# The last layer norm of a graph kernel moved from a closing block on VectorE into the tile loop on GpSimd

## The reference, cut to what matters

```python
h = relu(layernorm(x)); Xf = Xb = Xa = h; Z = 0
for s in range(2):                       # step zero and step one
    A = adj_from_feats(Xa, W1, W2, W3)   # logits, keep the top 0.9 of the softmax mass per row
    Xf, Xb, Xa = Rf @ Xf, Rb @ Xb, A @ Xa
    Z = Z + (Xf @ U1[s] + Xb @ U2[s] + Xa @ U3[s])
Y = h + Z
out = x + (Y - mean(Y)) / sqrt(var(Y) + 1e-5) * gamma + beta
```

## Time and profile before

| | us |
|---|---|
| median of 3 runs | 2197.3 (2192.13 to 2199.02) |
| the profiled execution, its own time | 2191.76 |
| its span, first to last instruction | 2190.0 |
| VectorE busy | 1913.4 (87%) |
| TensorE busy | 1880.3 (86%) |
| ScalarE busy | 1680.4 (77%) |
| GpSimd busy | 706.6 (32%) |

### The profile page before, as it was taken

The page is one execution under the profiler, slowest core; times in us unless marked ns, Lnnn a source line. Parts: engine busy times, 40 slices in busy tenths (PEclk is TensorE's granted clock), DMA queues, the critical chain, the costliest instruction groups (busy, mean ns, idle before and its releaser), DMA issues. The chain is left out here.

```text
span 2190.0 us, 32462 instructions
## 1 busy us (share of the span) xinstructions
PE 1880.3 (86%) x9866; PEld 1245.4 (57%) x9866; DVE 1913.4 (87%) x6109; ACT 1680.4 (77%) x1740; POOL 706.6 (32%) x1392
## 2 busy tenths in 40 slices
PE   1999963999999999999883898999899999999892
PEld 1555531666666666666661555666565656565662
DVE  6777788899889999988758999999999999999995
ACT  5444345899999999999824999898989898989940
POOL 2000042244443344444323333333333333333324
PEclk9999986999999999999995999999999999999996
DMA  6777621111111111111106001010101010101023
GB/s 218 284 284 283 217 95 44 38 39 50 54 54 51 55 55 37 52 54 51 55 29 237 21 26 41 23 44 23 44 23 44 23 44 23 44 23 44 22 91 122
DMA packets 65725, 167.61 MB, mean 77 GB/s; under 512 B 7037, under 2 KB 45307, under 8 KB 61947
## 3 DMA queue, kind: packets, MB, share of 16 engines
q1 hardware_dynamic: 65530, 165.43, 21.7%
HBM read 117.95 MB, written 47.45 MB: 76 GB/s over the span
## 5 line engine op out<-in xcount | busy, mean ns | idle before, releaser
L1449 PE MATMUL banks<-xa,pt 128*128 128x256 f32 x2704 | 636.4, 387 | 16.2 <-ACT pt L949 15.8
L1449 PEld LDWEIGHTS banks<-xa,pt 128*128 128x128 f32 x2704 | 501.7, 192 | 157.1 <-issue 71.3
L920 ACT ACTIVATE junk_a<-pb_all,minus_t 128x3327 f16<-128x3327 f32 x150 | 461.0, 3073 | 96.5 <-POOLq L843 93.8
L925 ACT ACTIVATE junk_a<-pb_all,minus_t 128x3327 f16<-128x3327 f32 x150 | 460.6, 3071 | 4.1
L1500 PE MATMUL banks<-region,at 128*128 128x512 f16 x2028 | 456.3, 380 | 0.0
L828 POOL TENSOR_SCALAR over<-over,points 128x1 f32<-128x1 f32 x150 | 96.8, 646 | 763.7 <-ACT junk_a L925 763.7
L1500 PEld LDWEIGHTS banks<-region,at 128*128 128x128 f16 x2028 | 196.4, 98 | 218.3 <-issue 2.1
L1375 PE MATMUL banks<-keys,qs 64*128 64x512 f32 (+1 forms) x816 | 191.2, 569 | 101.0 <-DMA qs<-q_d 31.8
L1241 DVE TENSOR_SCALAR_CACHE_REDUCE pb_all<-banks 128x1024 f32<-128x1024 f32 x260 | 209.3, 848 | 27.4 <-PE banks L1375 19.1
L1103 DVE MAX8 junk_v<-below 128x8 f32<-128x208 f32 (+1 forms) x624 | 222.4, 432 | 2.2
L949 ACT ACTIVATE pt<-banks 128x896 f32<-128x896 f32 x208 | 171.2, 859 | 61.4 <-PE banks L1441 61.2
(11 more groups left out here) (223 smaller groups left out, 2797.8 us busy)
## 6 DMA issues: line engine op xcount, KB each, us to landing
at<-adjT_d SPq DMA_DIRECT2D x52, 832.0 KB, 4.9
region<-in_adj_dram SPq DMA_DIRECT2D x25, 1663.5 KB, 8.0
adjT_d<-at SPq DMA_DIRECT2D x26, 832.0 KB, 3.9
fb_d<-fb_sb SPq DMA_DIRECT2D x26, 256.0 KB, 2.0
region<-fb_d SPq DMA_DIRECT2D x2, 3328.0 KB, 19.2
y_d<-y_sb SPq DMA_DIRECT2D x50, 128.0 KB, 1.7
x_d<-pb_all SPq DMA_DIRECT2D x1, 3328.0 KB, 11.0
qs<-q_d SPq DMA_DIRECT2D x104, 32.0 KB, 4.1
```

The lines of the kernel that those rows point to most:

```text
L920: nc.scalar.activation(junk_a[:, 0:w], pb[u][:, 0:w], ACT.Relu, scale=sign, bias=t, accum_out=over[u][:, 0:1])\
L925: nc.scalar.activation(junk_a[:, 0:w], pb[u][:, 0:w], ACT.Sign, scale=sign, bias=t, accum_out=over[u][:, 1:2])\
L1449: last = nc.tensor.matmul(bank[4][:, 0:D], pt[sl][:, t * P:(t + 1) * P], xa[:, t0 + t, :], start=(t0 + t == 0), stop=(t0 + t == T - 1))
```

## The change

Six edits go together.

1. VectorE: `add_z` in step one is followed by a wait on `y_stats` and a `bn_aggr` of that tile alone; `y_done` is raised by the latter.
2. GpSimd: `normalise(i-2)` stands behind `level(j, 4)` in body i: five linked one-column instructions, of which one is a power of -0.5 and the others a Newton step, then one 128x256 `tensor_scalar` that subtracts the mean and multiplies by the inverse deviation. `finish(i-3)` stands ahead of `level(j, 4)`: three 128x256 `tensor_tensor` instructions (residual plus beta, norm times gamma, their sum). One `memset` is added at the start of the step.
3. SP: per tile, `x1` of the tile is loaded from `x1_d` and the finished tile is stored to `out`. The load of step zero's Y stands one body later; the store to `y_d` in step one is gone.
4. SP: gamma and beta are loaded into `scales` (the memory of `fb_sb`) at the start of step one, ahead of the U matrices and the large feature loads.
5. The closing block is gone: VectorE's `finish`, ScalarE's two `Sqrt` instructions, GpSimd's 26 additions of beta, the large reloads and large stores.
6. The last tile is stored in two pieces after `store_out(T-2)`.

```diff
@@ sync, step one
+                def store_out(q):
+                    sp.wait_ge(S("out_sum"), q.t + 1)
+                    for r0, r1 in LAST_ROWS if q.t == T - 1 else [(0, P)]:
+                        sp.dma_start(out[q.t * P + r0:q.t * P + r1, :], n_t[q.slot][r0:r1, :]).then_inc(S2("out_stored")[q.slot], 16)
                     if not first and i.static and i.t == -2:
+                        for n, v in enumerate((gamma, beta)):
+                            sp.dma_start(scales[:, n, :], bc(v)).then_inc(sem("scale_in"), 16)
...
-                    if not first and i.inside(T):
-                        sp.wait_ge(S2("y_stored")[i.slot], 16 * i.use)
-                        sp.dma_start(y_sb[i.slot][:, :], y_d[dyn(i)]).then_inc(S2("y_loaded")[i.slot], 16)
+                    if not first and k.inside(T):
+                        if k.t >= 2:
+                            sp.wait_ge(S("n_done"), k.t - 1)
+                        sp.dma_start(y_sb[k.slot][:, :], y_d[dyn(k)]).then_inc(S2("y_loaded")[k.slot], 16)
+                        if k.t >= 2:
+                            sp.wait_ge(S("out_sum"), k.t - 1)
+                        sp.dma_start(x1_t[k.slot], x1_d[:, k.t * D:(k.t + 1) * D]).then_inc(S2("x1_loaded")[k.slot], 16)
+                    if not first and (i + -3).inside(T):
+                        store_out(i + -3)
...
@@ gpsimd
+                def normalise(q):
+                    pool.wait_ge(S2("y_done")[q.slot], q.use + 1)
+                    mean, var = mv[:, q.t, 0:1], mv[:, q.t, 1:2]
+                    v, root, h, r = (a[:, q.t:q.t + 1] for a in (ve, sd, lt, ly[:, :, 0]))
+                    ch.link(nc.gpsimd.tensor_scalar(v, var, EPS, None, ALU.add))
+                    ch.link(nc.gpsimd.tensor_tensor(root, v, minus_half[:, :], ALU.pow))
+                    ch.link(nc.gpsimd.tensor_scalar(h, root, root, v, ALU.mult, ALU.mult))
+                    ch.link(nc.gpsimd.tensor_scalar(h, h, -0.5, 1.5, ALU.mult, ALU.add))
+                    ch.link(nc.gpsimd.tensor_tensor(r, root, h, ALU.mult))
+                    pool.wait_ge(S2("out_stored")[q.slot], 16 * q.use_here)
+                    nc.gpsimd.tensor_scalar(n_t[q.slot], y_sb[q.slot][:, :], mean, r, ALU.subtract, ALU.mult).then_inc(S("n_done"), 1)
+
+                def finish(q):
+                    pool.wait_ge(S2("x1_loaded")[q.slot], 16 * (q.use_here + 1))
+                    pool.wait_ge(sem("scale_in"), 32)
+                    pool.wait_ge(S("n_done"), q.t + 1)
+                    ch.add(nc.gpsimd.tensor_tensor(x1_t[q.slot], x1_t[q.slot], scales[:, 1, :], ALU.add))
+                    ch.link(nc.gpsimd.tensor_tensor(n_t[q.slot], n_t[q.slot], scales[:, 0, :], ALU.mult))
+                    nc.gpsimd.tensor_tensor(n_t[q.slot], n_t[q.slot], x1_t[q.slot], ALU.add).then_inc(S("out_sum"), 1)
...
+                    if not first and 0 <= i.t - 3 < T - 2:
+                        finish(i + -3)
                     for e in range(EARLY if first else EARLY + 1, SUB + ACT_BISECTIONS[s] - 1):
                         level(j, e)
+                    if not first and (i + -2).inside(T):
+                        normalise(i + -2)
+                        if i.t >= T:
+                            finish(i + -2)
                     if not first:
                         level(m, 0)
...
@@ vector
-                        nc.vector.bn_stats(stats[:, k.t, :], y_sb[k.slot][:, :]).then_inc(S2("y_done")[k.slot], 1)
+                        nc.vector.bn_stats(stats[:, k.t, :], y_sb[k.slot][:, :]).then_inc(S("y_stats"), 1)
+                        dve.wait_ge(S("y_stats"), k.t + 1)
+                        nc.vector.bn_aggr(mv[:, k.t, :], stats[:, k.t, :]).then_inc(S2("y_done")[k.slot], 1)
```

More of the change, by code:

```diff
@@ L341, in sweep @@
             body(Idx(0, i, base, unroll))
-    OUT_GROUPS = [(t, 6) for t in range(0, T - 2, 6)]
     def dyn(i):
@@ L723, in diffusion_step @@
         nxt = Idx(0, 0, T, 6)
+        x1_t = [v[:, 0, :] for v in t256]
+        n_t = [v[:, 1, :] for v in t256]
+        EVEN = LAST - LAST % 16
+        LAST_ROWS = [(r0, r1) for r0, r1 in ((0, EVEN), (EVEN, LAST)) if r1 > r0]
         with nc.Block() as block:
@@ L762, in body @@
                         sp.dma_start(q_d[1, dyn(k)], qo[:, :]).then_inc(S("qo_stored"), 16)
-                    if k.inside(T) and (first or not k.static or k.t < T - 2):
+                    if first and k.inside(T):
                         sp.wait_ge(S2("y_done")[k.slot], k.use + 1)
                         sp.dma_start(y_d[dyn(k)], y_sb[k.slot][:, :]).then_inc(S2("y_stored")[k.slot], 16)
[L766 to L775, removed]
                 step_sweep(sp, body)
@@ L784, in _ @@
                 else:
[L785 to L795, removed]
+                    store_out(Idx(0, T - 1, T, 6))
+                    for u in range(2):
+                        sp.wait_ge(S2("out_stored")[u], 16 * (T // 2 + (len(LAST_ROWS) - 1 if u == (T - 1) % 2 else 0)))
             @block.gpsimd
@@ L848, in _ @@
                 ch = Chain(pool, f"step_levels_{s}")
+                if not first:
+                    ch.link(nc.gpsimd.memset(minus_half[:, :], -0.5))
                 def body(i):
@@ L882, in _ @@
                 step_sweep(pool, body)
[L883 to L887, removed]
             @block.scalar
@@ L1295, in settle @@
                     dve.sem_inc(S("masked"), 1)
[L1297 to L1301, removed]
-                    ch.wait()
-                    inverse_deviation(dve, 4 if t0 else 3, "out_chain", 6 if t0 else 0, 1.0, t0, t1)
-                    dve.wait_ge(sem("scale_in"), 32)
-                    for h, (u0, n) in enumerate(OUT_GROUPS if t0 == 0 else [(t0, t1 - t0)]):
-                        if t0 == 0:
-                            dve.wait_ge(sem("y_in"), 16 * len(OUT_GROUPS))
-                        for t in range(u0, u0 + n):
-                            y = y_sb[t % 2][:, :] if t0 else yall[:, t, :]
-                            nc.vector.scalar_tensor_tensor(out=yall[:, t, :], in0=y, scalar=mv[:, t, 0:1], in1=gamma_bc,
-                                                           op0=ALU.subtract, op1=ALU.mult).then_inc(sem("out_scaled"), 1)
-                        dve.wait_ge(sem("out_scaled"), u0 + n)
-                        dve.wait_ge(sem("x1_beta"), u0 + n)
-                        for t in range(u0, u0 + n):
-                            nc.vector.scalar_tensor_tensor(out=yall[:, t, :], in0=yall[:, t, :], scalar=ly[:, t, :], in1=x1_in[:, t, :],
-                                                           op0=ALU.mult, op1=ALU.add).then_inc(sem("out_done"), 1)
                 def coarse_search(j):
@@ L1347, in body @@
                             coarse_search(nxt)
-                    if not first and i.static and i.t == T - 1:
-                        for u in range(2):
-                            dve.wait_ge(S2("y_done")[u], T - 1)
-                        finish(0, T - 2)
                 step_sweep(dve, body)
-                if not first:
-                    for u in range(2):
-                        dve.wait_ge(S2("y_done")[u], T)
-                    finish(T - 2, T)
             @block.tensor
```

10 lines of the change are left out of this document (2 added, 8 removed).

## The result

The changed kernel takes 2171.95 us (median of four runs, 2170.07 to 2178.67) against 2197.85 us for the kernel before (median of four, 2192.13 to 2199.02). The ratio is 0.989, 95% interval 0.987 to 0.991; a later set, with six runs of the one and 17 of the other, gives 0.989 again, 0.987 to 0.991. The forecast was 2178.4, in a range from 2170 to 2192.

The account below looks back on a forecast made before the run. VectorE's own list was taken to set the tile's period of 37.0 us. Terms: -30.0 close, +9.6 loop, +0.6 body 25, +0.9 start = -18.9 us; 2197.3 - 18.9 = 2178.4 us, range 2170 to 2192.

Parts of the forecast that it names:

- the band of 2176 to 2183: Whole kernel: forecast case, each tile 0.3 to 0.6 us longer on VectorE; chance 0.55.
- the aggregation alone: Step one's loop: rival that the port costs nothing, 0.20 us per tile, 2173.6 us; chance with anything less 0.20.
- The close: End of step one: the last tile's own norm and store, 8.4 instead of 37.6 us; with 0.9 from `Sqrt`, 30.0 saved.
- VectorE, +0.20 a tile for the aggregation: Step one's loop: `bn_aggr` waits for `bn_stats` to end, so its successor starts 0.53 us behind `bn_stats` instead of 0.33.
- The port: Step one's loop: GpSimd's `normalise` holds up VectorE's small instructions on the shared SBUF port, 0.20 us per tile (0 to 1.0).
- body 25: Loop body without ScalarE passes, where GpSimd runs later and `finish` meets L1098: 0.6 us once.
- The start: Start of step one: gamma and beta issued ahead of loads that TensorE waits for, two issues, 0.9 us added.
- VectorE sets the pace: Step one's loop: VectorE's own list sets the tile's period, 37.0 us; anything added to it lengthens the tile.
- GpSimd's room of 2.3 us: Step one's loop: `normalise` may last 2.3 us longer at no cost before L867 meets VectorE's L1171.
- The rival of a long power: Step one's loop: the power takes 2.40 us and holds VectorE, 2.65 us per tile, 2234.5 us; chance 0.08.
- The time to which the sum was added: Forecast's base: median of the runs before, 2197.3 us; the profiled execution, 2191.76, lay 5.5 us under it.
- The whole-instruction hold: Step one's loop: rival that GpSimd holds the port for each whole instruction, 1.35 us per tile, 2201 us; chance 0.07.

Follow-up runs that it names:

- the late loads: Changed kernel with the gamma and beta loads moved from the head of step one's transfers to its first tile: 2176.07 us.
- the two runs with added work: Changed kernel plus, per tile, two short ScalarE copies (2170.31 us), or a second VectorE `bn_stats` into a spare tile (2179.65 us, ratio 0.993).
- the wait: VectorE's first long pass waits for GpSimd's second rough level of the next tile: kernel before 2192.46 us, changed kernel 2171.11 us.
- the run with nine powers: Changed kernel with the power of each tile's deviation issued nine times instead of once on GpSimd: 2320.87 us, ratio 1.056.

## Why the prediction came out as it did

The sum said 18.9 us less; the two profiled executions, neither with the hold in its second tile, differ by 20.6. The spans differ by 20.5: 29.6 less at the close, 8.3 more in the loop, 0.8 more at the start. So the mechanism and the terms held. The forecast of the time, 2178.4 us, was 6.4 too high, and the measured 2171.95 lies below the band of 2176 to 2183 that the prediction held likeliest, in the one given to the aggregation alone, though the 0.30 us a tile are within the likeliest. That is the fault of the time that the sum was added to, the last point below; the range was wide enough for it.

- **The close, 30.0 predicted.** 29.6 measured, from the end of the last subtraction on VectorE to the end of the span (58.57 to 28.95 us). The rows inside are off in places: the five narrow instructions take 2.0 us instead of 1.85, because the power takes 0.58; the wide one 1.25 instead of 0.92, plus 0.17 of handing over; the last three 2.2 instead of 2.4. The first product of the last tile waits 0.24 us, so its 0.9 were there.
- **VectorE, +0.20 a tile for the aggregation.** 0.18, by the run without it; in the list the next instruction starts 0.22 later. Right.
- **The port, +0.20 a tile.** 0.12, by the run that moves the wide instruction. Right in kind: a one-input GpSimd instruction costs VectorE a short delay once, and the row it was taken from (L873, +0.15) was the right neighbour. The 0.05 set aside for the narrow ones can't be seen: beside the power L1146, with two inputs, takes 0.15 us.
- **Together 9.6 us in the loop and 0.6 in body 25.** 8.3: 24 x 0.30 = 7.2, and some 1.0 in body 25, where `finish` meets L1094 (0.69 for 0.15), L1097 (0.34 for 0.22) and L1115 (4.04 for 3.68). The terms of the loop were too large by 0.1 us a tile, 2.4 us in all; the 0.4 too much at the close and the 0.4 too little in body 25 take that down to the 1.6 us between the sum and the spans.
- **The start, 0.9.** 0.84 by the two profiled executions, and the late loads take it back; but the start differs by up to 2.2 us between profiled executions with the same loads ahead, so the sign is shown and the size only roughly.
- **VectorE sets the pace.** Shown by the two runs with added work.
- **GpSimd's room of 2.3 us.** This step was wrong, though nothing hung on it here. I counted GpSimd's half of the subtraction as free until VectorE's half begins. It was 1.8, since `normalise` takes 3.3 us and not the 2.8 that the sum of its rows gave. Two more microseconds already brought the overlap (0.69 us, VectorE's half +0.54), because the half also slips when the level ahead of it does. And beyond it the price isn't the lateness of one instruction: with 5.4 us more the tile grows by up to 9.7 us instead of the 2.5 expected. The rival of a long power had the wrong path. It let VectorE stand for the length of the power, 2.65 us a tile at 2.1 us of power more; with 2.0 more no VectorE instruction beside the powers is longer, and the tile grows by 0.4. The price comes only when GpSimd's later instructions slip into VectorE's long ones.
- **The time to which the sum was added.** The prediction went from the median of three runs, 2197.3, and called the profiled execution 5.5 us below it. That difference was not noise to be carried over: it was the hold in the second tile, which by their times the kernel before meets in 24 of all its 37 runs, and the changed one in 2 of 10. (No profiled execution of either lies in its upper group; that it is this hold is read from the three traces of other versions and from what the wait does.) 2197.3 - 18.9 = 2178.4 is where the changed kernel lies when it meets it (2178.67, 2177.90); its median doesn't. With the wait in both, the medians differ by 21.35 us.

The whole-instruction hold fell as the rule for GpSimd's norm. The Trainium skill, "SBUF — State Buffer", section "SBUF: two separate sides", has the engine that comes second stand until the first has finished, where VectorE's instruction has two inputs in SBUF and GpSimd's reads SBUF. The rows agree where VectorE's long instruction has two inputs and comes first (L857, 3.59 us) and where both engines' are long and have two (L1189, 3.08). L850 stood though it began 0.04 us first, which may be too little to tell the order by. They don't agree for the wide `tensor_scalar` L816, one input and 1.25 us: four two-input VectorE instructions run beside it, and only the first is longer, by 0.12 to 0.15.

What stays open: why the changed kernel meets the hold less often than the one before, and with it whether those 5.3 us of the medians are chance or an effect of the change. The margin between the end of GpSimd's level and the start of VectorE's pass doesn't tell: it is 0.25 us in the profiled execution of the kernel before (L838 ends at 1255.10 and L1089 begins at 1255.35), 0.03 and 0.23 in two of the changed one. Nor does the start: the version with the late loads, whose first product began at 1193.22, met the hold in three of four runs, but the one with the second `bn_stats` began at 1192.94 and met it in none of four, and the hold is in a trace that began at 1194.02. Open too is the one run of twelve at 2196.34.

## What to carry over

An engine that sets the pace pays for what is put into its list only where it isn't waiting: the same 0.18 us a tile cost 4.5 us in one place and nothing some 14 us further down the list, behind the last long instruction and ahead of a wait. When runs of one kernel fall into two groups, compare a trace of each, or of a near version, before the median is used as a base; here the difference was a fifth of what the change seemed to bring. And where a short instruction of one engine stands just ahead of a long one of another on the same port, a wait on the long one's side cost 0.6 us in the second tile here and saved the hold.

## What the runs showed of the hardware that was not expected

A GpSimd instruction on 128x1, 0.27 us alone, lasts 3.59, 3.46 or 3.09 us when it begins beside a VectorE `scalar_tensor_tensor` over 128x3327 (3.69 us); L850, which began 0.04 us ahead of VectorE's half of the subtraction (2.54 us), lasts 2.62 in the run with nine powers. Each ends with VectorE's, within 0.15 us. The power of 128x1 takes 0.57 to 0.63 us on GpSimd in the changed kernel; the `tensor_scalar` with two operations over 128x256 takes 1.25 us at its least, where L873 with one took 0.92. On VectorE, `scalar_tensor_tensor` over 128x256 takes 0.48 us, so that the last tile's two such steps replaced three GpSimd instructions of 0.72 to 1.25; the fourth, `x1` plus beta, stays on GpSimd and is done ahead. And a hold of 3.3 us on one of GpSimd's small instructions, with a second of 2.8 on the next level's (L847, 3.09 us), became 7.4 us on VectorE: TensorE idled for 5.39 us in between and came back at a granted clock of 0.69 and 0.63.
